# Two hybrid expert-attention layers on one core: the heads' output is routed by one two-factor product per head, and the low parts of the values are made by GpSimd in half units

## The reference, cut to what matters

```
def _L1_ffn_ref(x, Wq, Wkv, Ws, Wd, Wo):
    H, E, DH, K = (8, 5, 64, 3)
    ss = sigmoid(x @ Ws).reshape(b, t, H, E);  sd = sigmoid(x @ Wd).reshape(b, t, H, E)
    ms = _topk_mask(ss, K);  md = _topk_mask(sd, K)
    q = einsum('bthed,bthe->bhtd', q5, sd * md)
    k = einsum('bthed,bthe->bhtd', k5, ss * ms)
    v = einsum('bthed,bthe->bhtd', v5, ss * ms)
    attn = softmax(einsum('bhid,bhjd->bhij', q * scale, k), axis=-1)
    out = einsum('bhij,bhjd->bihd', attn, v)
    o5 = einsum('bthd,dm->bthm', out, Wo).reshape(b, t, H, E, DIM)
    return einsum('bthem,bthe->btm', o5, md)
```

## Time and profile before

| | |
|---|---|
| median of 3 runs | 2662.1 us (2661.57 to 2664.65) |
| the profiled execution's own time | 2660.86 us |
| its span in the trace | 2659.0 us |
| busy, share of the span | PE 89%, PEld 57%, DVE 77%, ACT 56%, POOL 67% |
| the two changed stages' steps in the trace | about 1389 to 1920 us, and 2102 to 2634 us |

### The profile page before, as it was taken

How to read it: one execution, slowest core, us unless ns; L and a number is a source line. 1 busy time by engine, 2 the same in 40 slices (tenths; PEclk the granted TensorE clock), 3 DMA queues, 4 the chain that set the end, 5 groups by cost and what they waited for, 6 DMA issues and landing times. The chain is left out here.

```text
span 2659.0 us, 55314 instructions
## 1 busy us (share of the span) xinstructions
PE 2357.8 (89%) x21054; PEld 1521.2 (57%) x21054; DVE 2034.9 (77%) x3668; ACT 1478.0 (56%) x2069; POOL 1783.3 (67%) x1676
## 2 busy tenths in 40 slices
PE   6788777887799999999979999999879799999987
PEld 3555534644466666666655666665634466666655
DVE  7998545545677777777679999998577999999983
ACT  4222122332788888888924556665653255566564
POOL 0888200000899999999947888888710478888885
PEclk9899779988899999999989999999989999999997
DMA  1000000001699998989924656666610256666665
GB/s 45 1 1 0 1 24 14 1 24 53 117 166 148 158 160 151 161 152 154 150 83 87 112 110 114 112 114 118 124 32 0 70 112 112 112 112 115 116 119 107
DMA packets 829351, 243.47 MB, mean 92 GB/s; under 512 B 811528, under 2 KB 820232, under 8 KB 829088
## 3 DMA queue, kind: packets, MB, share of 16 engines
q1 hardware_dynamic: 829088, 239.93, 49.0%
HBM read 20.70 MB, written 1.05 MB: 8 GB/s over the span
## 5 line engine op out<-in xcount | busy, mean ns | idle before, releaser
L2292 PE MATMUL banks<-g_w,normed_t 128*128 128x320 f32 x1536 | 508.3, 457 | 47.8 <-DVE g_scratch L2592 34.0
L1582 POOL TENSOR_TENSOR g_p_lo<-g_p,g_p_hi 128x768 bf16<-128x768 f32 (+1 forms) x256 | 478.2, 1889 | 34.9 <-POOL g_z L2482 22.3
L1775 DVE TENSOR_REDUCE at_negmax<-banks 128x1 f32<-128x1024 f32 x256 | 301.6, 1220 | 152.9 <-PE banks L1687 152.9
L2292 PEld LDWEIGHTS banks<-g_w,normed_t 128*128 128x128 f32 x1536 | 261.6, 189 | 237.6 <-DVE g_scratch L2592 115.0
L1752 POOL TENSOR_TENSOR at_p_lo<-at_p,at_p_hi 128x640 bf16<-128x640 f32 x256 | 356.1, 1408 | 13.4 <-ACT at_p_hi L1740 11.7
L1595 DVE TENSOR_REDUCE g_negmax<-banks 128x1 f32<-128x1024 f32 x256 | 310.1, 1217 | 40.7 <-PE banks L1505 40.5
L1559 ACT ACTIVATE g_p<-banks,g_negmax 128x1024 f32<-128x1024 f32 x256 | 284.9, 1113 | 9.1 <-DVE g_negmax L1595 8.8
L1733 ACT ACTIVATE at_p<-banks,at_negmax 128x1024 f32<-128x1024 f32 x256 | 285.4, 1115 | 6.3 <-DVE at_negmax L1775 6.3
L1687 PE MATMUL banks<-at_k_t,at_q 64*128 64x512 f32 x1024 | 257.0, 620 | 18.1 <-POOL at_k_t L2036 10.0
L1505 PE MATMUL banks<-g_k_t,g_q 64*128 64x512 f32 x1024 | 256.2, 619 | 16.9 <-ACT g_p L1559 10.4
L1572 ACT CAST g_r_hi<-banks 128x256 bf16<-128x256 f32 x128 | 47.6, 372 | 396.5 <-PE banks L1516 396.5
(11 more groups left out here) (419 smaller groups left out, 5996.0 us busy)
## 6 DMA issues: line engine op xcount, KB each, us to landing
at_swapped<-at_crossed SPq DMA_DIRECT2D x128, 128.0 KB, 2.7
g_w<-in_ex_w SPq DMA_DIRECT2D x2, 2880.0 KB, 11.5
f_w<-in_W SPq DMA_DIRECT2D x2, 1024.0 KB, 5.6
at_rope<-in_rope SPq DMA_DIRECT2D x1, 2048.0 KB, 9.6
at_t_hi<-at_p_hi SPq DMA_TRANSPOSE x128, 3.6
at_t_lo<-at_p_lo SPq DMA_TRANSPOSE x128, 3.6
g_t_hi<-g_p_hi SPq DMA_TRANSPOSE x128, 4.2
g_t_lo<-g_p_lo SPq DMA_TRANSPOSE x128, 4.2
```

The lines of the kernel that those rows point to most:

```text
L1582: self.nc.gpsimd.tensor_tensor(self.part(self.p_lo, j, h), self.p[:, j % 2, h, 0:self.WIDTH[h]], self.part(self.p_hi, j, h), ALU.subtract) ...
L1775: self.nc.vector.tensor_reduce(self.negmax[:, j % 2, h:h + 1], self.core.banks[:, first:first + 2, :], AX.XY, ALU.max, negate=True).then_i ...
L2292: nc.tensor.matmul(out[:, 0:ED], core.xt[:, at:at + P], w[:, kind * H + tile // (T * BATCH) * 2 + h, :], start=True, stop=True).then_inc(p ...
```

## The change

Routing: `share` is gone. `dve_route` makes the reciprocal and then, for each head, one `scalar_tensor_tensor` of 128 x 320: output x reciprocal (a value per partition) x kept.

Values: the split of a unit is cut in two halves of four tiles (128 x 520). ACT makes half 0 of the next unit at t = 4, as soon as its four tiles are summed, and half 1 of the current unit at t = 0. POOL makes the low part of each, right behind the low parts of the probabilities in the same steps. DVE makes only those of unit 0, ahead of the loop. `sum_values` now waits at t = 0 for half 0 of the current unit (made four steps earlier), and at t = 4 for half 1.

```
--- before.py
+++ after.py
@@ -1468,7 +1468,6 @@
         self.r_hi, self.r_lo = (sb(n, [P, 2, self.KEPT * P], BF16) for n in ("r_hi", "r_lo"))
         self.minus = sb("minus", [P, P], BF16)
         self.recip = sb("recip", [P, 2])
-        self.share = sb("share", [P, 2, 5])
         self.routed = sb("routed", [P, 2, 2, 5, 64])
         self.ones_ready = sem("ones_ready")
         self.s_full = sem("s_full")
@@ -1480,7 +1479,7 @@
         self.r_turned, self.r_copied = sem("r_turned"), sem("r_copied")
         self.minus_ready, self.r_full, self.r_split = sem("minus_ready"), sem("r_full"), sem("r_split")
         self.av_done = sem("av_done")
-        self.recip_ready, self.share_ready = sem("recip_ready"), sem("share_ready")
+        self.recip_ready = sem("recip_ready")
         self.o_ready = sem("o_ready")
         self.v_split_hi = sem("v_split_hi")
         self.v_split = sem("v_split")
@@ -1532,7 +1531,7 @@
             if j:
                 pe.wait_ge(self.o_ready, j)
             if j % self.T == 0:
-                pe.wait_ge(self.v_split, j // self.T + 1)
+                pe.wait_ge(self.v_split, 2 * (j // self.T) + 2)
         at = (j % 2) * 130 + h * 65
         for k in range(self.T):
             n = k - self.WIDTH[0] // P
@@ -1601,21 +1600,33 @@
         o = self.sums[:, at:at + 130].rearrange("p (h c) -> p h c", h=2)
         self.nc.vector.reciprocal(self.recip[:], o[:, :, 64]).then_inc(self.recip_ready, 1)
         dve.wait_ge(self.recip_ready, j + 1)
-        self.nc.vector.tensor_tensor(self.share[:], kept, self.core.col(self.recip[:], 5), ALU.mult).then_inc(self.share_ready, 1)
-        dve.wait_ge(self.share_ready, j + 1)
         if j >= 2:
             dve.wait_ge(added, j - 1)
-        self.nc.vector.tensor_tensor(self.routed[:, j % 2], o[:, :, 0:64].unsqueeze(2).to_broadcast([P, 2, 5, 64]),
-                                     self.share[:].unsqueeze(3).to_broadcast([P, 2, 5, 64]), ALU.mult).then_inc(self.o_ready, 1)
-
-    def act_split_values(self, act, unit, ready):
+        for h in range(2):
+            ins = self.nc.vector.scalar_tensor_tensor(out=self.routed[:, j % 2, h], in0=o[:, h, 0:64].unsqueeze(1).to_broadcast([P, 5, 64]),
+                                                      scalar=self.recip[:, h:h + 1], in1=kept[:, h].unsqueeze(2).to_broadcast([P, 5, 64]),
+                                                      op0=ALU.mult, op1=ALU.mult)
+        ins.then_inc(self.o_ready, 1)
+
+    def half(self, i):
+        return slice(self.T // 2 * i, self.T // 2 * (i + 1))
+
+    def act_split_values(self, act, unit, i, ready):
         act.wait_ge(*ready)
         act.wait_ge(self.ones_ready, 1)
-        self.nc.scalar.copy(self.v_hi[:, unit % 2], self.v[:]).then_inc(self.v_split_hi, 1)
-
-    def dve_split_values(self, dve, unit):
-        dve.wait_ge(self.v_split_hi, unit + 1)
-        self.nc.vector.tensor_tensor(self.v_lo[:, unit % 2], self.v[:], self.v_hi[:, unit % 2], ALU.subtract).then_inc(self.v_split, 1)
+        if unit >= 2:
+            act.wait_ge(self.av_done, 2 * self.T * (unit - 1))
+        self.nc.scalar.copy(self.v_hi[:, unit % 2, self.half(i)], self.v[:, self.half(i)]).then_inc(self.v_split_hi, 1)
+
+    def pool_split_values(self, pool, unit, i):
+        pool.wait_ge(self.v_split_hi, 2 * unit + i + 1)
+        self.nc.gpsimd.tensor_tensor(self.v_lo[:, unit % 2, self.half(i)], self.v[:, self.half(i)], self.v_hi[:, unit % 2, self.half(i)],
+                                     ALU.subtract).then_inc(self.v_split, 1)
+
+    def dve_split_values(self, dve, unit, i):
+        dve.wait_ge(self.v_split_hi, 2 * unit + i + 1)
+        self.nc.vector.tensor_tensor(self.v_lo[:, unit % 2, self.half(i)], self.v[:, self.half(i)], self.v_hi[:, unit % 2, self.half(i)],
+                                     ALU.subtract).then_inc(self.v_split, 1)
 
 
 class TransferStream:
@@ -2433,7 +2444,8 @@
             for h in range(2):
                 hs.act_exp(act, 0, h)
                 hs.act_hi(act, 0, h)
-            hs.act_split_values(act, 0, (v_ready, T))
+            for i in range(2):
+                hs.act_split_values(act, 0, i, (v_ready, T // 2 * (i + 1)))
             for j in range(STEPS):
                 unit, t = j // T, j % T
                 last = j + 1 == STEPS
@@ -2446,7 +2458,9 @@
                 if not last:
                     hs.act_hi(act, j + 1, 0)
                 if t == 0 and unit:
-                    hs.act_split_values(act, unit, (v_ready, (unit + 1) * T))
+                    hs.act_split_values(act, unit, 1, (v_ready, (unit + 1) * T))
+                if t == 4 and unit + 1 < UNITS:
+                    hs.act_split_values(act, unit + 1, 0, (v_ready, (unit + 1) * T + T // 2))
                 if not last:
                     hs.act_exp(act, j + 1, 1)
                 hs.act_rest(act, j)
@@ -2523,6 +2537,10 @@
             for j in range(STEPS):
                 for h in range(2):
                     hs.pool_lo(pool, j, h)
+                if j % T == 0 and j:
+                    hs.pool_split_values(pool, j // T, 1)
+                if j % T == 4 and j // T + 1 < UNITS:
+                    hs.pool_split_values(pool, j // T + 1, 0)
                 if j < 18 and j % 9 < 8:
                     count_duels(2 + j // 9, j % 9)
                 elif j < 18:
@@ -2593,8 +2611,8 @@
                                     own.unsqueeze(2).to_broadcast([P, 2, D, E]), ALU.mult).then_inc(product_ready, 1)
 
             def sum_values(tile):
-                if tile % T == 0 and tile:
-                    dve.wait_ge(hs.v_split, tile // T)
+                if tile % 4 == 0 and tile >= T:
+                    dve.wait_ge(hs.v_split, tile // 4 - 1)
                 dve.wait_ge(product_ready, (last_of(tile, 2) + 1) // 2)
                 v.tensor_reduce(hs.v[:, tile % T, :, 0:D], v_product[:, tile % 2], AX.X, ALU.add).then_inc(v_ready, 1)
 
@@ -2652,7 +2670,8 @@
                 if tile > T:
                     sum_keys(tile - 1)
                 else:
-                    hs.dve_split_values(dve, 0)
+                    for i in range(2):
+                        hs.dve_split_values(dve, 0, i)
                 apply_gates(n + 2, 6)
             sum_keys(LEAD - 1)
             for j in range(STEPS):
@@ -2673,8 +2692,6 @@
                 if unit + 1 == UNITS and t > 2:
                     add_out(*done_in(t - 1)[1])
                 beside(1)
-                if t == 0 and unit:
-                    hs.dve_split_values(dve, unit)
                 if j + T < TOTAL:
                     sum_values(j + T)
                 if j:
```

8 lines of the change are left out of this document (2 added, 6 removed).

## The result

| | before | with the change |
|---|---|---|
| median of the runs | 2661.84 us (2661.55 to 2664.65, 4 runs) | 2644.35 us (2640.06 to 2650.02, 4 runs) |
| ratio of the medians | | 0.9933, 95% interval 0.9915 to 0.9951 |
| profiled execution, its span | 2660.86 us, 2659.0 us | 2640.06 us, 2638.3 us |

The change saves 17.5 us where the forecast said 12, and the time lies inside the range.

What follows compares the result with a forecast made beforehand. PE's chain of projections, products and scores was taken to bound the step. Per stage, 10.8 (boundaries) + 1.5 (share's waits) + 1.5 (unit 7) - 7.8 (POOL's lag) = 6.0 us, 12 for two stages: 2650 us, range 2637 to 2664.

Steps and rivals of the forecast that it cites:

- What bounds the kernel: Ordinary step of 7.72 us: PE's chain of projections, products and scores sets it, and DVE follows with next to no slack.
- the boundaries: Step t = 0 of units 1 to 6: falls from 9.51 to 7.72 us, 1.8 us each, 10.8 per stage.
- New waits of `sum_values`: Sum of values at t = 0 and t = 4: waiting for the halves counted at nothing; without cover, 1.8 us again.
- Routing: DVE's path from reciprocal to K: 1.11 us in place of 1.14, worth nothing while PE bounds.
- the share's waits: Share on DVE, mean 238 ns against 0.17 us: its waiting goes, counted as 1.5 us saved per stage.
- POOL's lag: Low parts on POOL delay t_lo: PE stalls about 0.6 us at t = 2 and 6, 13 halves, -7.8 us a stage.
- Unit 7: Last unit, without projections: ACT's wait at t = 0 falls 0.5 us and t_lo's stall 1.0, 1.5 per stage.
- A: POOL's idle time and t_lo's slack absorb the halves, PE never stalls: 2634 us; chance 0.17.
- B: POOL becomes the bound, a half costing nearly 2.165 us there and stalling PE 1.6 through t_lo: 2676 us; chance 0.10.
- C: Unit 7 takes the gain back: stall over 2 us moves to another step, clock falls, 4 to 5 us a stage: 2659; chance 0.14.
- D: Routing is dearer at 0.54 us a product: DVE late 0.06 to 0.1 in about 100 steps, 2658 us; chance 0.09.

## Why the prediction was right, and where its terms were off

**What bounds the kernel, and the boundaries.** Right. Six boundaries gave 11.7 us a stage for 10.8 forecast. The difference is unit 2, whose t = 0 took 10.77 and not 9.51: I had multiplied one unit's step by six without looking at the others.

**New waits of `sum_values` at nothing.** Right in the change; the kernel with both halves at t = 0, where the sum waits 0.91, shows that the distance between half and reader does it.

**Routing.** The path is 1.12 us for 1.11 forecast, neutral, and the share's waits were worth 0.7 a stage at t = 4 and with the small falls in units 0 and 1 some 1.5, as forecast. What I missed is the link between the parts: the new split lengthens the waits of the old share, so the split without the new routing would have earned only 10.5. Together with the split the routing is worth 17.5 - 10.5 = 7 us by the medians. The terms were summed as if independent, with the share's waits measured beside the old POOL program.

**POOL's lag.** The mechanism is right: place (t = 2 and 6), releaser (t_lo), POOL's half (1174 ns for 1167), start of the next low parts (V + 8.00 for 8.08). The term was mis-sized: 3.3 us a stage in place of 7.8. First, the lateness of t_lo against the wanted V + 0.02 is 0.52 in unit 5, but the step grows by 0.37, because in the long step PE has work of its own beside part of the wait (its idle is only 0.36). Second, I charged all 13 halves. In units 1 and 2 the step t = 2 stayed at 8.32 to 8.33, and in units 0 and 1 t = 6 grew by 0.07 to 0.16, but for the one long step. In the first two units POOL adds one product less to the sums (one `g_z` instruction of 0.86 in a step for two), and has slack that unit 4, from which I took the 7.58, does not have. The first stage bears it out: the low parts of t = 1 begin 0.20 and 0.10 us ahead of their step's V in units 1 and 2, and 0.29 behind it in units 3, 5 and 6. So 8 halves pay 0.4 each. The kernels with half 0 at t = 5 show the third side of it: the price of a half depends on the step between it and the use.

**Unit 7.** Forecast 1.5 a stage, measured 5.8 and 4.9 in the trace. The stall of 2.46 with the clock at 0.50 behind it is gone; the longest idle for t_lo in unit 7 of the first stage is now 1.29. The split took it away: with the routing alone it is still 2.45, with the split alone 1.74, and with unit 7's split back on DVE 2.05. The split is worth 1.5 us a stage by that last kernel, and 2.0 and 2.8 by the one with the split alone, where unit 7 takes 51.0 and 50.6. The kernel with the routing alone takes 49.9 and 50.3, about 3 less than before, but not by a stall that the routing removed. In the first stage the kernel before had one more stall, of 1.62, behind a t_lo that landed after 5.88 us, and the step is 9.79 for 6.56 without it. In the second both have the stall (2.99 and 2.90), and only the clock behind it differs: before, it stayed at 0.50 for 9 us, and the scores ran slowly:

```profile
2603.25 3.79 PE L1505 MATMUL banks<-g_k_t,g_q 64*128 64x512 f32 x8
```

With the routing alone it was back at 1.00 after 3:

```profile
2601.83 1.99 PE L1504 MATMUL banks<-g_k_t,g_q 64*128 64x512 f32 x8
```

I had allowed for some us either way here; whether the routing has a part in these 3 us, or whether they come and go between executions, one profile of each does not tell. The rest of the program was 4.2 us longer in the profiled execution with the routing alone than in the one before, so that its stages fell by 8.0 and its time by 3.9.

**What was not in the sum: single long steps.** Three of 12, 9.97 and 8.79 us. In the longest (second stage, unit 6, t = 2) PE's timeline reads:

```profile
2518.05 1.34 PE L2303 MATMUL banks<-g_w,normed_t 128*128 128x320 f32 x4
2521.92 0.24 PE L1545 MATMUL banks<-g_v_hi,g_t_hi 128*128 128x65 bf16 x1 [2.31 <-DMA g_t_lo<-g_p_lo]
2523.24 2.23 PE L2303 MATMUL banks<-g_w,normed_t 128*128 128x320 f32 x4
```

The t_lo that was issued at 2516.03, and its time to landing:

```profile
2516.03 1.52 SPq L1590 DMA_TRANSPOSE g_t_lo<-g_p_lo  x1
...
g_t_lo<-g_p_lo SPq DMA_TRANSPOSE x1, 5.8
```

Stretches around it (us, busy by engine, granted clock, DMA share, GB/s):

```profile
2518.00:2521.90 3.90, 1.62 (x8) 0.96 (x6) 3.39 (x4) 1.39 (x2) 3.58 (x4) 0.97 1.18 133
2521.90:2525.00 3.10, 3.08 (x28) 2.50 (x29) 0.00 (x0) 1.85 (x2) 2.94 (x4) 0.50 0.47 102
```

The landing took 5.8 us in place of 4.2, PE stood for 2.31 with nothing in hand, and then ran at the lower clock, 0.50, with 2.23 for a pair of 1.34. The kernel before has landings of up to 5.9 too, and the one with the routing alone had one of 4.9 near this place, with its steps as long as ever; there t_lo came early enough. With the half a step later the same step took 12.38 us (12.33 in the repeat), with both halves at t = 0 12.10, with the low parts left out 8.32. In the repeat of the change t_lo landed after 4.45 there and the step took 9.22. I take it that POOL's lag has used up the slack of t_lo, so that a slow landing now reaches PE, with the clock's fall added to it. This fits the spread of the runs too (2640 to 2650 with the change, 2627.8 to 2631.4 with the low parts left out), but no run varied the landing on purpose.

The traces do show what slow landings go with. While the t_lo of 2516.03 was under way, one packet of another queue ran beside the transposes; in the transfers from 2515.9 to 2522.0:

```profile
q1 hardware_dynamic: 2727, 0.69, 89.9%
q8 instruction: 1, 0.02, 1.0%
```

It is one of 16 KB, and it began 3.9 us after the issue. The traces of the twelve kernels here hold 1536 transfers of t_lo. With 993 of them no packet of an instruction queue was under way in the 4.2 us after the issue, and none took over 4.3 us. With the other 543 one was, and 221 of these took 4.4 to 6.3; where it had begun ahead of the issue, in 182 cases, none was late. So the slow landings are not scattered at random: they return near the same place in the change and its repeat (5.75 and 5.92 in unit 0, which gives the steps of 9.97 and 10.14). That the packet is the cause is not shown by a run that moves it.

So the forecast's 12 is a sum with errors of both signs: in two stages, 9 us too much for POOL's lag, 2 too little at the boundaries, some 8 too little in unit 7 by the trace, and 6.5 of long steps that it did not have. With these it comes to 24, which is what the stages of the profiled execution show (23.6), and not to the 17.5 of the medians. The mechanism was forecast, the nearness of the number is in part luck: a term more than twice too large stood against two that were too small or missing.

**The rivals.** A (no stall) fell: the stall is there, but at 3.3 of the forecast's 7.8 a stage the time lies about halfway to A's 2634. B fell by its price, 1.17 and not 2.17 a half, and its mechanism was shown by the kernel with the low parts twice. C appeared outside unit 7, as the long steps. D fell: 0.47 from product to product, and the other steps did not grow, but for t = 5 of unit 6 (6.72 to 6.84) and the long steps.

## What to carry to other kernels

When work moves to another engine, follow what that engine feeds two steps on, and place the moved piece so that the slack of a longer step lies between it and the use of what it delays: one step later was worth 6.5 to 8.5 us here by the medians. Measure the interaction of two edits by running each alone, since a small operation with two SBUF inputs can wait behind work that the other edit moves or shifts. And read a repeated step in every unit before multiplying one of them.
